# Attention rounds of a graph kernel: ten-tile stretches over three PSUM banks in place of chunks of up to four tiles

## The chip, the cores and the metric

The kernel runs on one core of one Trainium2 chip, as a single launch. The time is the device time of that launch in microseconds. Four engines take part in the stage that is changed: VectorE (DVE) does the arithmetic, GpSimd (POOL) issues the gathers, ScalarE (ACT) does the exponentials and the index arithmetic, SyncE (SP) resets signals. TensorE is idle there.

## The reference

Four graph layers follow each other over 6250 nodes of 128 features and 106250 edges (50000 drawn edges in both directions and one self loop per node): two SAGE convolutions with batch norm, a Moebius-addition scan, an equivariant convolution and a graph attention layer, with a layer norm after each. The change lies in the last one:

```python
h = (x @ W_lin).reshape(n, H, C)                    # H = 4 heads of C = 32
alpha = a_src[src2] + a_dst[dst2] + a_e
alpha = jnp.where(alpha >= 0, alpha, NEG * alpha)
m = jax.ops.segment_max(alpha, dst2, num_segments=n)
ex = jnp.exp(alpha - m[dst2])
denom = jax.ops.segment_sum(ex, dst2, num_segments=n)
w = ex / denom[dst2]
msg = h[src2] * w[:, :, None]
out = jax.ops.segment_sum(msg, dst2, num_segments=n)
```

and after it bias, residual and two layer norms.

## The kernel before

The function `gat` computes this layer in the last fifth of the launch (from about 5776 us). The nodes lie in 49 tiles of 128, one node per partition. The nodes were ordered so that those with many edges stand in the first tiles. The tiles form eight groups of 1, 4, 4, 8, 10, 9, 7 and 6 (`SIZES`), and `UPTO` holds their running sums 1, 5, 9, 17, 27, 36, 43, 49.

The work goes in turns. In one turn every node takes its next edge: POOL gathers one row of 136 floats (128 of `h`, the attention terms behind them) per node, one indirect DMA per tile, into `rows[:, r]`. There are two such buffers, r = 0 and 1, which alternate from turn to turn. As nodes run out of edges the turns get shorter: a phase p works on the first T = UPTO[p] tiles, from 49 down to 1. In the profiled execution there were twelve turns of 49 tiles, two each of 43, 36, 27, 17 and 9, four of 5 and ten of 1, which makes 882 gathers. After the phases of 49, 43, 36 and 27 tiles the group that has just ended is finished (`finish`: the self loop, division, two layer norms), on DVE and ACT.

Within a turn DVE (`turn`) first computes the scores of the gathered edges and the running maximum in small instructions (L2637 to L2649), ACT takes two exponentials into PSUM (`ex`: the factor for the old sums and the weight of the new edge), and DVE then updates `acc`, the running sum of messages. This is done in chunks of up to four tiles within a group (`CHUNKS`): 15 of them for 49 tiles. Each chunk takes three wide instructions: L2668 multiplies the old sum in `acc` by `ex[0]`; L2669 multiplies the gathered rows by `ex[1]` and writes one PSUM bank of six (`ps[:, 1 + c % 6]`); L2661 (`add_up`) adds that bank to `acc`. `add_up` of a chunk is issued one chunk later, after the two products of the next one, and waits for the signal of its own L2669.

Signals set the order. `gathered[r][g]` counts the gathers of a group, and DVE waits for all groups of the phase before a turn. `idx_ready[r]` tells POOL that ACT has the indices of the next turn in this buffer. `consumed[r][g]`, one per buffer and group, is raised by the last L2669 of a group; POOL waits for it before it gathers that group of the next turn into the same buffer (L2535 to L2539). SP clears these signals and raises each once at the start. A helper, `Chain`, raises a signal of its own after an instruction and waits for it where the next one depends on it (`do(...)` does both, `do.put` only the first).

Of the kernel before, what the change touches and what calls it, by code (L numbers as in the profile page):

```python
# [21 lines left out]
ALU = mybir.AluOpType  # L22
# [6 lines left out]
D = 128  # L29
TILES = -(-N // P)  # L30
# [33 lines left out]
NG = len(SIZES)  # L64
# [3 lines left out]
CHUNKS_TO = tuple(sum(1 for c in CHUNKS if c[0] <= g) for g in range(NG))  # L68
# [2372 lines left out]
def gat(nc, a, t, s, out):  # L2441
# [4 lines left out]
    with ExitStack() as ctx:  # L2446
# [11 lines left out]
        idx = sb("idx", [P, 2, TILES], I32)  # L2458
        MOST = max(SIZES)
        FINISH = [(g, 0, PART[g]) for g in range(NG - 1, 2, -1)] + [(0, 1, slice(0, UPTO[2]))]  # L2460
        INSIDE = NG - 4
# [28 lines left out]
        gathered = [[sem(f"gathered{r}_{g}") for g in range(NG)] for r in range(2)]  # L2490
        consumed = [[sem(f"consumed{r}_{g}") for g in range(NG)] for r in range(2)]
        scattered = sem("scattered")
# [6 lines left out]
        @block.sync  # L2499
        def _(sp):  # L2500
            for r in range(2):
                for g in range(NG):
                    sp.sem_inc(consumed[r][g], 1)
            sp.dma_start(own_row[:], t["own"].rearrange("(t p) f -> p t f", p=P)).then_inc(nodes_in, 16)
            for tile, name in ((bias, "bias"), (gain, "ln_g"), (shift, "ln_b")):
                sp.dma_start(tile[:], a["L3_gnn_" + name].partition_broadcast(P)).then_inc(w_in, 16)
            with sp.Fori(0, span_count(sp, s)) as c:
                sp.wait_ge(arrived, 3 * c + 3)
                sp.sem_inc(took, 1)
                for x in (*per_span, *consumed[0], *consumed[1]):  # L2510
                    sp.sem_clear(x)  # L2511
                for r in range(2):
                    for g in range(NG):
                        sp.sem_inc(consumed[r][g], 1)  # L2514
                sp.sem_inc(go, 1)

        @block.gpsimd
        def _(pool):
# [8 lines left out]
            with pool.Fori(0, span_count(pool, s)) as c:  # L2527
                for p, lo, hi in phases(turn_counts(pool, s)):
                    with pool.Fori(lo, hi) as b:
                        for r in range(2):  # L2530
                            pool.wait_ge(idx_ready[r], b + 1)
                            pool.sem_inc(took, 1)
                            for g in range(p + 1):
                                pool.wait_ge(consumed[r][g], b + 1)
                                pool.sem_inc(took, 1)  # L2535
                                for n in range(PART[g].start, PART[g].stop):
                                    pool.indirect_dma_start(rows[:, r, n, :], None, flat,  # L2537
                                                            bass.IndirectOffsetOnAxis(ap=idx[:, r, n:n + 1], axis=0)
                                                            ).then_inc(gathered[r][g], 16)  # L2539
# [75 lines left out]
        def _(dve):  # L2615
# [9 lines left out]

            last = [c for c, x in enumerate(CHUNKS) if c + 1 == len(CHUNKS) or CHUNKS[c + 1][0] != x[0]]

            def turn(before, p, b, r):
# [23 lines left out]
                do(dve.tensor_tensor(ex[:, 1, 0:T], ex[:, 1, 0:T], valid4, ALU.mult))  # L2652
                made = {}

                def add_up(c):
                    g, lo, hi = CHUNKS[c]
                    if c in last:
                        dve.wait_ge(consumed[r][g], b + 2)
                    else:
                        dve.wait_ge(do.sem, made[c])  # L2660
                    return dve.tensor_tensor(acc[:, lo:hi], acc[:, lo:hi],  # L2661
                                             ps[:, 1 + c % 6, 0:(hi - lo) * D].rearrange("p (u d) -> p u d", d=D), ALU.add)

                for c in range(CHUNKS_TO[p]):
                    g, lo, hi = CHUNKS[c]
                    wide = [P, hi - lo, heads, cols]
                    mine = acc[:, lo:hi].rearrange(by_head, c=cols)
                    dve.tensor_tensor(mine, mine, ex[:, 0, lo:hi].unsqueeze(3).broadcast_to(wide), ALU.mult)  # L2668
                    weighted = dve.tensor_tensor(ps[:, 1 + c % 6, 0:(hi - lo) * D].rearrange("p (u h c) -> p u h c", h=heads, c=cols),  # L2669
                                                 rows[:, r, lo:hi, 0:D].rearrange(by_head, c=cols),  # L2670
                                                 ex[:, 1, lo:hi].unsqueeze(3).broadcast_to(wide), ALU.mult)
                    if c in last:
                        weighted.then_inc(consumed[r][g], 1)
                    else:
                        do.put(weighted)
                        made[c] = do.n
                    if c == 0:
                        dve.tensor_tensor(dn, dn, ex[:, 1, 0:T], ALU.add)
                    else:
                        add_up(c - 1)  # L2680
                do(add_up(CHUNKS_TO[p] - 1))

# [157 lines left out]
```

## Time and profile before

| What | Value |
|---|---|
| Median of three runs | 7172.02 us (7158.86 to 7176.2) |
| The profiled execution | 7217.74 us, its span 7216.0 us |
| DVE busy over the span | 3417.0 us, 9467 instructions |
| POOL busy over the span | 4476.8 us, 4570 instructions |
| L2668, L2669 and L2661 | 278 instructions each |
| L2537, the gathers | 882, 851.9 us busy |

How to read it: busy time is the time in which an engine executes; time in which an instruction waits for a signal stands as idle time before it. The profile names what ended such a wait by the signal that moved last, so a signal that an earlier stage used under another name can be called by that stage's name (`mb_rows`, `eq_xrow`), and "remote" and "issue" mean that no instruction of the profile was found for it. All times within the span count from the first instruction.

### The profile page before, as it was taken

Reading aid. Unit: us, or ns where it says so; the run is one execution under the profiler, and the core shown is the slowest. Engines: PE = TensorE matmul, PEld = TensorE weight load, DVE = VectorE, ACT = ScalarE, POOL = GpSimd, SP = SyncE. Lnnn points to the kernel's source line nnn. Section 1 sums busy time; section 2 is a strip of 40 time slices with the busy share of each in tenths; the row PEclk is TensorE's granted clock in tenths of the full one; section 3 lists DMA queues with packets and bytes.
Section 4 is the critical chain, followed back from the end, with each engine's and each line's share of the span. In section 5 each row is a group of like instructions: output and inputs, shape, how many; then the busy total and the mean of one; then the engine's idle time right before and its main releaser. Section 6 shows DMA issues by size and latency. Waiting matters only on the chain. (4 is left out here: it accounts for less than half of the span.)

```text
span 7216.0 us, 54797 instructions
## 1 busy us (share of the span) xinstructions
PE 2423.7 (34%) x12640; PEld 1803.1 (25%) x12640; DVE 3417.0 (47%) x9467; ACT 1775.5 (25%) x5753; POOL 4476.8 (62%) x4570
## 2 busy tenths in 40 slices
PE   5786665465566550000000024555555300000000
PEld 4565555344444430000000012333333200000000
DVE  2333333333434363566677865555544333434466
ACT  1111111111111010222333246766666200000011
POOL 5666666566766656566665436666666577667545
PEclk7767767677778775555555557777777655555555
DMA  3333333765555523121211113333333232122111
GB/s 100 99 102 99 99 102 100 174 189 168 167 165 163 164 72 78 40 47 43 47 43 43 29 63 90 88 95 96 97 94 95 83 89 52 45 49 52 39 34 37
DMA packets 404902, 637.30 MB, mean 88 GB/s; under 512 B 148580, under 2 KB 248966, under 8 KB 404340
## 3 DMA queue, kind: packets, MB, share of 16 engines
q0 software_dynamic: 175664, 424.09, 22.4%
q1 hardware_dynamic: 139076, 115.67, 6.0%
q10 hardware_dynamic: 89856, 94.18, 4.0%
q8 instruction: 104, 1.70, 0.1%
q14 instruction: 202, 1.65, 0.1%
HBM read 529.65 MB, written 103.93 MB: 88 GB/s over the span
## 5 line engine op out<-in xcount | busy, mean ns | idle before, releaser
L1590 POOL DMA_INDIRECT mb_rows<-x_tab,mb_idx x882 | 834.4, 946 | 594.1 <-ACT mb_ps L1638 299.5
L2537 POOL DMA_INDIRECT gt_rows<-h_tab,gt_idx x882 | 851.9, 966 | 499.9 <-issue 274.0
L977 POOL DMA_INDIRECT s_rows<-y_split,srcS x824 | 857.2, 1040 | 425.9 <-issue 223.0
L2040 POOL DMA_INDIRECT eq_ring<-fx_tab,srcS x824 | 820.9, 996 | 452.8 <-issue 236.2
L555 POOL DMA_INDIRECT s_rows<-in_x,srcS x824 | 782.1, 949 | 449.6 <-issue 221.2
L2075 ACT ACTIVATE eq_ring<-eq_ring 128x64 f32<-128x64 f32 x3328 | 861.9, 336 | 459.4 <-issue 364.2
L2116 PE MATMUL eq_ps<-eq_ring,eq_onehot 128*128 128x320 f32 x1664 | 627.3, 537 | 627.1 <-issue 394.8
L2116 PEld LDWEIGHTS eq_ps<-eq_ring,eq_onehot 128*128 128x128 f32 x1664 | 381.3, 239 | 851.7 <-issue 781.8
L1700 PE MATMUL mb_ps<-ident,mb_rows 128*128 128x128 f32 x49 | 11.3, 332 | 1576.2 <-ACT mb_rows L1667 1575.3
L1055 PE MATMUL s_ps<-s_onehot,s_rows 128*128 128x128 bf16 x4992 | 444.4, 250 | 199.5 <-issue 177.6
L194 DVE TENSOR_TENSOR s_onehot<-iota,dstM 128x512 bf16<-128x512 f32 x206 | 142.4, 692 | 755.6 <-remote 389.9
L194 DVE TENSOR_TENSOR s_onehot<-s_ps,dstM 128x512 f32<-128x512 f32 x206 | 141.9, 689 | 716.9 <-PE s_ps L630 431.1
L1055 PEld LDWEIGHTS s_ps<-s_onehot,s_rows 128*128 128x128 bf16 x4992 | 380.2, 114 | 286.0 <-issue 247.6
L629 PE MATMUL s_ps<-s_onehot,s_rows 128*128 128x128 f32 x1664 | 424.5, 390 | 1.6 <-DVE s_onehot L194 1.6
L1638 ACT ACTIVATE mb_ps<-mb_rows,mb_gm 128x128 f32<-128x128 f32 x882 | 260.9, 351 | 601.0 <-DVE mb_gm L1789 524.5
L1700 PEld LDWEIGHTS mb_ps<-ident,mb_rows 128*128 128x128 f32 x49 | 6.8, 154 | 1580.8 <-issue 1573.6
L629 PEld LDWEIGHTS s_ps<-s_onehot,s_rows 128*128 128x128 f32 x1664 | 365.8, 260 | 61.8 <-issue 22.4
L2661 DVE TENSOR_TENSOR gt_acc<-gt_acc,gt_ps 128x128 f32<-128x128 f32 (+3 forms) x278 | 158.6, 574 | 400.3 <-remote 171.4
L1749 DVE TENSOR_TENSOR mb_prod<-mb_ps,mb_xf 128x256 f32<-128x256 f32 (+3 forms) x278 | 276.1, 1000 | 127.0 <-issue 36.3
L1741 DVE TENSOR_REDUCE mb_both<-mb_prod 128x2 f32<-128x256 f32 (+3 forms) x278 | 275.4, 994 | 61.2 <-DVE mb_prod L1749 29.6
L1804 DVE SCALAR_TENSOR_TENSOR mb_xf<-mb_xf,mb_v,mb_ps 128x128 f32<-128x128 f32 x882 | 247.8, 343 | 101.5 <-issue 51.7
L194 DVE TENSOR_TENSOR eq_onehot<-eq_ps,dstM 128x512 f32<-128x512 f32 x206 | 141.6, 687 | 317.9 <-remote 228.9
(505 smaller groups left out, 5484.1 us busy)
## 6 DMA issues: line engine op xcount, KB each, us to landing
w_tab<-s_wrow ACTq DMA_DIRECT2D x208, 264.0 KB
eq_ring<-w_tab SPq DMA_DIRECT2D x208, 264.0 KB
s_es<-in_side ACTq DMA_DIRECT2D x208, 136.0 KB
mb_rows<-x_tab,mb_idx POOLq DMA_INDIRECT x882
gt_rows<-h_tab,gt_idx POOLq DMA_INDIRECT x882
s_rows<-in_x,srcS POOLq DMA_INDIRECT x824
s_rows<-y_split,srcS POOLq DMA_INDIRECT x824
eq_ring<-fx_tab,srcS POOLq DMA_INDIRECT x824
```

Of the source, the lines that this page charges most:

```text
L194: return dve.tensor_tensor(onehot[:, 4 * half:4 * half + 4], broadcast(numbers, four, 1), broadcast(columns, four, 2), ALU.is_equal)
L555: pool.indirect_dma_start(rows[:, n % SLOTS, :], None, a["x"], bass.IndirectOffsetOnAxis(ap=s["srcS"][:, n:n + 1], axis=0)).then_inc(gathe ...
L629: pe.matmul(ps[:, bank, 0:P], rows[:, slot], onehot[:, u], start=(u == 0), stop=(u == U - 1))
L977: pool.indirect_dma_start(rows[:, n % SLOTS, :], None, t["ys"], bass.IndirectOffsetOnAxis(ap=s["srcS"][:, n:n + 1], axis=0)).then_inc(gath ...
L1055: last = pe.matmul(ps[:, 2 * bank + f, 0:P], rows[:, slot, at:at + P], onehot[:, u], start=(u == 0 and part == 0), stop=(u == U - 1 and pa ...
L1590: pool.indirect_dma_start(rows[:, r, n, :], None, t["x1"], bass.IndirectOffsetOnAxis(ap=idx[:, r, n:n + 1], axis=0)).then_inc(gathered[r][ ...
L1741: do.put(dve.tensor_reduce(both[:, :, lo:hi], prod[:, c % 3, :, 0:hi - lo], AX_X, ALU.add))
L1749: dve.tensor_tensor(prod[:, c % 3, :, 0:hi - lo], copied(c).unsqueeze(1).broadcast_to(wide), xf[:, :, lo:hi, 0:D], ALU.mult).then_inc(mult ...
L2040: pool.indirect_dma_start(frow[:, n % SLOTS, :], None, features, bass.IndirectOffsetOnAxis(ap=s["srcS"][:, n:n + 1], axis=0)).then_inc(gat ...
L2075: last = act.activation(pb[:, r % 2, u, f].rearrange("p c w -> p (c w)"), wrow[:, r, u, lo:lo + 64], ACT.Copy, scale=wrow[:, r, u, D + f:D ...
L2116: last = pe.matmul(ps[:, bank, 0:MC], onehot[:, 4 * h + u], msg[:, h, u], start=(h == 0 and u == 0), stop=(h == 1 and u == 3))
L2537: pool.indirect_dma_start(rows[:, r, n, :], None, flat, bass.IndirectOffsetOnAxis(ap=idx[:, r, n:n + 1], axis=0)).then_inc(gathered[r][g], 16)
```

## The change

It concerns `turn` and the signals it shares with POOL and SP. In place of the 15 chunks a turn has stretches of ten tiles (`RUN`), regardless of the groups: five for 49 tiles, the last of nine. A stretch takes three PSUM banks, 1 to 3 or 4 to 6 in turn. The order of the three wide instructions stays as it was; in each the operand in PSUM now stands first. `consumed` is kept per stretch, not per group, and every L2669 raises it; POOL waits for it before the first tile of each stretch. From the third stretch on, the product into PSUM waits until the addition of the stretch before last, which read the same banks, is done.

```diff
+        RUN = 10
+        RUNS = -(-TILES // RUN)
...
-        consumed = [[sem(f"consumed{r}_{g}") for g in range(NG)] for r in range(2)]
+        consumed = [[sem(f"consumed{r}_{c}") for c in range(RUNS)] for r in range(2)]
...
                             for g in range(p + 1):
-                                pool.wait_ge(consumed[r][g], b + 1)
-                                pool.sem_inc(took, 1)
                                 for n in range(PART[g].start, PART[g].stop):
+                                    if n % RUN == 0:
+                                        pool.wait_ge(consumed[r][n // RUN], b + 1)
+                                        pool.sem_inc(took, 1)
...
-                made = {}
-
-                def add_up(c):
-                    g, lo, hi = CHUNKS[c]
-                    if c in last:
-                        dve.wait_ge(consumed[r][g], b + 2)
-                    else:
-                        dve.wait_ge(do.sem, made[c])
-                    return dve.tensor_tensor(acc[:, lo:hi], acc[:, lo:hi],
-                                             ps[:, 1 + c % 6, 0:(hi - lo) * D].rearrange("p (u d) -> p u d", d=D), ALU.add)
-
-                for c in range(CHUNKS_TO[p]):
-                    g, lo, hi = CHUNKS[c]
+                runs = [(c, c * RUN, min(c * RUN + RUN, T)) for c in range(-(-T // RUN))]
+                weights = lambda c, many: ps[:, 1 + 3 * (c % 2):4 + 3 * (c % 2), :].rearrange("p b n -> p (b n)")[:, 0:many * D]
+
+                def add_up(c, lo, hi):
+                    dve.wait_ge(consumed[r][c], b + 2)
+                    do.put(dve.tensor_tensor(acc[:, lo:hi], weights(c, hi - lo).rearrange("p (u d) -> p u d", d=D),
+                                             acc[:, lo:hi], ALU.add))
+                    added[c] = do.n
+
+                added = {}
+                for c, lo, hi in runs:
                     wide = [P, hi - lo, heads, cols]
                     mine = acc[:, lo:hi].rearrange(by_head, c=cols)
-                    dve.tensor_tensor(mine, mine, ex[:, 0, lo:hi].unsqueeze(3).broadcast_to(wide), ALU.mult)
-                    weighted = dve.tensor_tensor(ps[:, 1 + c % 6, 0:(hi - lo) * D].rearrange("p (u h c) -> p u h c", h=heads, c=cols),
-                                                 rows[:, r, lo:hi, 0:D].rearrange(by_head, c=cols),
-                                                 ex[:, 1, lo:hi].unsqueeze(3).broadcast_to(wide), ALU.mult)
-                    if c in last:
-                        weighted.then_inc(consumed[r][g], 1)
-                    else:
-                        do.put(weighted)
-                        made[c] = do.n
+                    dve.tensor_tensor(mine, ex[:, 0, lo:hi].unsqueeze(3).broadcast_to(wide), mine, ALU.mult)
+                    if c >= 2:
+                        dve.wait_ge(do.sem, added[c - 2])
+                    dve.tensor_tensor(weights(c, hi - lo).rearrange("p (u h c) -> p u h c", h=heads, c=cols),
+                                      ex[:, 1, lo:hi].unsqueeze(3).broadcast_to(wide),
+                                      rows[:, r, lo:hi, 0:D].rearrange(by_head, c=cols), ALU.mult).then_inc(consumed[r][c], 1)
                     if c == 0:
                         dve.tensor_tensor(dn, dn, ex[:, 1, 0:T], ALU.add)
                     else:
-                        add_up(c - 1)
-                do(add_up(CHUNKS_TO[p] - 1))
+                        add_up(*runs[c - 1])
+                add_up(*runs[-1])
+                do.sync()
```

SP clears and raises the new list of signals in the same two places as the old one.

## Rows read from the trace of the kernel before

**Rows 1.** The page's engine shares: busy us, share of the span, instructions.

```profile
PE 2423.7 (34%) x12640; PEld 1803.1 (25%) x12640; DVE 3417.0 (47%) x9467; ACT 1775.5 (25%) x5753; POOL 4476.8 (62%) x4570
```

**Rows 2.** Waits of POOL, 5776 to 7216: us in total, times, longest.

```profile
POOL gt_rows L2537 <- issue: 274.0, 851, 8.9
POOL gt_rows L2537 <- DVE gt_ps L2669: 158.9, 13, 36.2
POOL gt_rows L2537 <- DMA mb_rows<-x_tab,mb_idx: 59.3, 15, 14.1
```

**Rows 3.** Stretches, one per turn or finish: limits, length, busy us (instructions), clock, DMA.

```profile
6159.90:6242.00 82.10, 0.00 (x0) 0.00 (x0) 28.36 (x59) 0.70 (x2) 47.95 (x50) 0.50 0.19 42
6522.30:6562.40 40.10, 0.00 (x0) 0.00 (x0) 26.85 (x59) 2.07 (x3) 22.46 (x24) 0.50 0.18 41
6627.00:6710.30 83.30, 0.00 (x0) 0.00 (x0) 28.25 (x59) 0.50 (x1) 62.33 (x66) 0.50 0.24 55
6710.30:6740.30 30.00, 0.00 (x0) 0.00 (x0) 13.34 (x49) 4.47 (x11) 0.00 (x0) 0.50 0.01 2
6740.30:6765.40 25.10, 0.00 (x0) 0.00 (x0) 23.75 (x53) 4.09 (x10) 14.18 (x15) 0.50 0.17 39
6765.40:6817.80 52.40, 0.00 (x0) 0.00 (x0) 24.71 (x53) 0.46 (x1) 39.75 (x42) 0.50 0.24 56
6817.80:6857.00 39.20, 0.00 (x0) 0.00 (x0) 14.91 (x53) 4.84 (x12) 14.18 (x15) 0.50 0.12 29
6857.00:6878.70 21.70, 0.00 (x0) 0.00 (x0) 20.20 (x47) 4.29 (x11) 11.88 (x13) 0.50 0.16 38
6919.40:6954.60 35.20, 0.00 (x0) 0.00 (x0) 18.01 (x61) 5.58 (x14) 8.52 (x9) 0.50 0.08 20
6954.60:6972.60 18.00, 0.00 (x0) 0.00 (x0) 15.56 (x38) 4.83 (x13) 8.61 (x10) 0.50 0.14 31
6972.60:6994.40 21.80, 0.00 (x0) 0.00 (x0) 15.82 (x38) 0.35 (x1) 16.62 (x18) 0.50 0.25 58
6994.40:7029.10 34.70, 0.00 (x0) 0.00 (x0) 19.54 (x65) 5.91 (x15) 6.95 (x8) 0.50 0.07 16
```

**Rows 4.** The same view, two stretches of POOL's gathers.

```profile
5811.97:6027.20 215.23, 0.00 (x0) 0.00 (x0) 67.59 (x145) 4.92 (x8) 162.97 (x172) 0.50 0.24 56
6027.30:6089.90 62.60, 0.00 (x0) 0.00 (x0) 20.49 (x43) 0.28 (x1) 49.10 (x45) 0.50 0.21 50
```

**Rows 5.** DVE in order of time, a slow turn: start, us, instruction, idle before.

```profile
6085.72 0.36 DVE L2645 TENSOR_TENSOR span_src<-span_src,gt_limit 128x196 f32<-128x196 f32 x1 [2.85 <-remote]
6087.12 0.36 DVE L2646 TENSOR_TENSOR span_src<-span_src 128x196 f32<-128x196 f32 x1 [1.04 <-issue]
...
6106.73 0.69 DVE L2661 TENSOR_TENSOR gt_acc<-gt_acc,gt_ps 128x512 f32<-128x512 f32 x1 [2.31 <-DMA mb_rows<-x_tab,mb_idx]
6107.33 0.68 DVE L2668 TENSOR_TENSOR gt_acc<-gt_acc,gt_ps 128x512 f32<-128x512 f32 x1
6107.93 0.69 DVE L2669 TENSOR_TENSOR gt_ps<-gt_rows,gt_ps 128x512 f32<-128x512 f32 x1
6110.23 0.69 DVE L2661 TENSOR_TENSOR gt_acc<-gt_acc,gt_ps 128x512 f32<-128x512 f32 x1 [1.60 <-issue]
```

**Rows 6.** The same view, in a finish: three instructions of 1280 elements.

```profile
7008.23 1.50 DVE L2723 TENSOR_TENSOR gt_ps<-gt_acc,gt_ps 128x1280 f32<-128x1280 f32 x1 [0.40 <-DVE gt_ps L2722]
7009.64 1.48 DVE L2725 TENSOR_TENSOR gt_rows<-gt_own_row,gt_ps 128x1280 f32<-128x1280 f32 x1
7011.15 1.50 DVE L2727 TENSOR_TENSOR gt_ps<-gt_ps,gt_rows 128x1280 f32<-128x1280 f32 x1
```

**Rows 7.** The first gathers, and DVE's first instruction on gathered rows.

```profile
5780.74 0.99 POOL L2537 DMA_INDIRECT gt_rows<-h_tab,gt_idx  x1 [8.89 <-issue]
...
5800.83 7.09 POOL L2537 DMA_INDIRECT gt_rows<-h_tab,gt_idx  x1 [0.30 <-issue]
...
5849.74 0.36 DVE L2640 TENSOR_TENSOR span_src<-gt_rows,edges_in 128x196 f32<-128x196 f32 x1 [30.89 <-DMA gt_rows<-h_tab,gt_idx]
```

More of the change, by code:

```diff
@@ L2501, in _ @@
             for r in range(2):
-                for g in range(NG):
-                    sp.sem_inc(consumed[r][g], 1)
+                for c in range(RUNS):
+                    sp.sem_inc(consumed[r][c], 1)
             sp.dma_start(own_row[:], t["own"].rearrange("(t p) f -> p t f", p=P)).then_inc(nodes_in, 16)
@@ L2512, in _ @@
                 for r in range(2):
-                    for g in range(NG):
-                        sp.sem_inc(consumed[r][g], 1)
+                    for k in range(RUNS):
+                        sp.sem_inc(consumed[r][k], 1)
                 sp.sem_inc(go, 1)
@@ L2624, in _ @@
             by_head = "p u (h c) -> p u h c"
-            last = [c for c, x in enumerate(CHUNKS) if c + 1 == len(CHUNKS) or CHUNKS[c + 1][0] != x[0]]
             def turn(before, p, b, r):
```

## The prediction

> **What bounds the kernel now.** I read the engine shares first. Over the whole span DVE is busy 47% and POOL 62% [rows 1], which says nothing of the last stage, where alone the change lies. So next come the waits of POOL inside that stage (5776 to 7216 us). Its 882 gathers wait 274.0 us for "issue", which is the fixed 0.3 us between two gathers. The other two rows are the ones to see: 158.9 us for L2669 and 59.3 us under the name of a transfer of an earlier stage [rows 2]. By the code a gather waits only for `idx_ready` and `consumed`, so most of these 218 us is POOL waiting for DVE to release row buffers.
>
> Third comes the table of stretches, one per turn [rows 3]. A turn of 49 tiles is 59 DVE instructions with 27 to 28 us of busy time. It took 82.1 us at 6160, as in seven of the twelve such turns to within 2 us, and 40.1 us in the one at 6522. The same work, twice the time: DVE is not busy, it is held. POOL needs 49 gathers of 1.2513 us (215.23 us for 172, [rows 4]), 61.3 us a turn. So the slow turns are set by DVE, the fast ones would be set by POOL.
>
> Fourth, DVE's own sequence shows where it is held: always at an instruction that waits for one of DVE's own signals [rows 5]. The addition at 6106.73 runs 0.60 us and the next two follow at 0.60 us each. Then the addition at 6110.23 starts after 1.60 us idle, though the product it waits for had ended long before. The spacing tells the price: 3.50 us for three instructions of 0.69 us there, 1.40 us for one instruction of 0.36 us at L2645. Over the slow turn it is 82.1/59 = 1.39 us per instruction, at 6627 83.3/59 = 1.41 us. So in this state the signals come back at a rate of one instruction per 1.4 us, whatever its length. Three instructions of 1280 elements follow each other 1.41 and 1.51 us apart with no idle time before them [rows 6]: an instruction that lasts 1.4 us pays nothing extra.
>
> **The change part by part.** *Fewer, wider instructions.* A turn of 49 tiles has 15 chunks, each with three wide instructions, 45 in all. Now it has five stretches (ten, ten, ten, ten, nine tiles), 15 instructions; the 14 others stay. 29 instructions at 1.40 us are 40.6 us in the held state. Not held, the 30 that go save only their fixed part: 512 elements are 0.60 us apart [rows 5], 1280 elements 1.41 us [rows 6], so 0.81 us for 768 elements, and 0.60 - 512 x 0.81/768 = 0.06 us is fixed; 30 x 0.06 = 1.8 us off 40.1 us. Either way the turn takes about 40 us, under POOL's 61.3 us.
>
> *What is late next.* POOL. Its first gather starts at 5780.74, one early gather takes 7.09 us, 6.1 us more than the others, and DVE starts its turn some 2.8 us after the start of the last gather (the 49th starts at 5780.74 + 48 x 1.2513 + 6.1 = 5846.9, L2640 at 5849.74) [rows 7]. Twelve turns of 49 are 588 gathers; without waiting for DVE the last starts at 5780.74 + 587 x 1.2513 + 6.1 = 6521.4 and the twelfth turn can start at 6524 instead of 6627: 103 us.
>
> *From there on* I follow both engines [rows 3]. The twelfth turn takes 40.6 us instead of 83.3 us and ends at 6565; the finish of the first group (30.0 us, not touched) ends at 6595. Two turns of 43 tiles: the first (25.1 us, less 24 x 0.06) ends at 6619, but the gathers of the second end only at 6521.4 + 86 x 1.2513 + 2.8 = 6632. It takes 29 x 1.40 = 40.6 us (52.4 us before), its finish 39.2 us: 6712. Two turns of 36 (14 + 12 instructions): POOL is ready at 6722, the first ends at 6712 + 20.4 = 6732, the second at 6769, its finish (35.2 us) at 6804. Two turns of 27: 17.1 and 20.9 us, finish 34.7 us: 6877, where it was 7029.1. That is 152 us. The turns of 17 to 5 tiles lose 42 instructions in all, 2.5 us, which I leave out against the releases below; those of one tile keep theirs.
>
> *POOL's own slow stretch.* From 6027 to 6090 45 gathers took 62.6 us, 1.39 us each [rows 4], after 215 us without a pause. Nothing in the rows tells why. POOL will now run for 740 us without a pause, so I charge one such stretch per 278 us, 2.7 x 45 x 0.14 = 17 us. At both ends: none, and all gathers (rival one).
>
> *Coarser releases.* `consumed` is now signalled per ten tiles, the first after two instructions of 1280 elements (2.8 us) instead of two of 128 (0.5 us or less). In turns of 49 POOL is a whole buffer behind these signals, 61.3 us against 40.6 us, so this is hidden; if that cover is gone it costs 2.3 us at each of the 28 waits of [rows 2]. In the eight turns of 17 to 5 tiles, where POOL and DVE alternate, it costs 0 to 2 us each; I take nothing, set against the 2.5 us.
>
> *Operand order, three banks.* The PSUM operand goes from second to first. L2723 and L2725 have it second, L2727 has it first: 1.50, 1.48 and 1.50 us for 1280 elements over three banks [rows 6]. Nothing, within 0.02 us x 15 a turn either way. The new wait for the bank of the stretch before last has a 1.4 us product issued in front of it and only the product behind it; held, it is one of the 29 instructions already counted. Six signals fewer to clear and set on SP: outside the turns, nothing.
>
> Sum: 152 - 17 = 135 us off the profiled execution's 7217.7 us (span 7216.0 us): 7083 us. The median of the runs, 7172.0 us, lies 45.7 us under it; with that difference kept it is 7037 us, and I say 7040 us. If the 45.7 us are delays that the timed runs never had, the gain is smaller by up to as much, 7083 us.
>
> One rule speaks against this. The row shows a wait for the own signal costing 1.0 to 2.3 us idle [rows 5]. The Trainium skill (VectorE: DVE Perf Modes, The DRAIN you can't avoid) says that a semaphore after each instruction costs nothing beyond the drain and that only the count of instructions matters, by their fixed part. By that the sum would be rival two's; the rows of this stage disagree.
>
> **The rivals.** *One: POOL falls to 1.39 us for good.* For: it did so in one long unpaused stretch [rows 4]. Against: it came back without a pause. The last gather of 49 tiles then starts at 5780.74 + 587 x 1.39 + 6.1 = 6602.8, the second turn of 43 at 6725, and by the same steps the finish after the turns of 27 ends near 6969: 60 us off, 7112 us.
>
> *Two: the hold does not go with the number of instructions* but with POOL's gathers beside it, so slow turns stay near 80 us. For: the turn at 6522 began after POOL had paused. Against: short and long instructions pay the same 1.4 us. Then only the fixed part goes, 1.8 us in seven slow turns of 49 and 10 us in the later ones (162 instructions): 7149 us.
>
> *Three: the hold belongs to the recording.* Starts after waits lie 0.70 us or a multiple apart (1.40 and 3.50 us, [rows 5]), as if timed by a clock outside the kernel. Then the timed runs are set by POOL already, and the change gains 10 us in the late turns: 7162 us. Against: without the hold the profiled execution would be well over 100 us shorter, yet it is only 45.7 us above the runs. The Trainium skill (NOTIFIC — the notification-queue block, 7.1) says that the block which writes trace records holds its producers back rather than lose a record; no run here shows whether it does.
>
> *Four, slower: the releases decide.* If slow turns stay as in rival two and POOL's restarts lie on the path, each of the 28 waits lengthens by 2.3 us, 64 us, less the 23 us of rival two: 7213 us. It decides from the point where a turn of DVE takes longer than POOL's 61.3 us. Against: 29 instructions would each have to cost over 2.1 us.
>
> **How the numbers follow.** Forecast 0.60 (7005 to 7085), rival one 0.20, two 0.08, three 0.06, four 0.06. The range 7005 to 7125 holds the first two, 0.80. About 0.3%, 21.5 us, can be told from no change. Faster: the first two and most of two, 0.86. Same: three and the rest of two, 0.08. Slower: four, 0.06.
>
> **What would show it.** Right: turns of 49 tiles 61 to 62 us apart, 29 DVE instructions in each, no idle time of POOL for L2669's successor before the last gather of 49 tiles, and the first finish starting near 6565 us. Wide instructions 1.4 us apart, without idle time before the additions. Rival one shows in a mean gather spacing near 1.39 us; two in turns still near 80 us with idle time before the five additions; three in a profile much faster than before and a median that has hardly moved; four in pauses of POOL at every first tile of a turn. The prediction is wrong if DVE turns of 49 tiles still take longer than 61 us.

## The result and the profile after

Over seven runs each the kernel after takes 7121.57 us (7111.88 to 7139.59), the kernel before 7161.19 us (7146.09 to 7176.2): ratio 0.9946, interval 0.9932 to 0.996, a gain of 39.6 us. I had forecast 7040 us (7005 to 7085), 132 us below 7172. The direction was right, the size three times too large.

The two profiles, 7216.0 and 7117.8 us long, are 98.2 us apart, more than the runs. The gathers show why. These are the first gathers of the last stage, first in the profile of after, then in a later profile of the same kernel (start, us, instruction, idle before):

```profile
5725.62 0.99 POOL L2540 DMA_INDIRECT gt_rows<-h_tab,gt_idx  x1 [8.91 <-issue]
```

```profile
5774.69 0.99 POOL L2540 DMA_INDIRECT gt_rows<-h_tab,gt_idx  x1 [8.93 <-issue]
```

Before starts there at 5780.74 [rows 7]. So 55.1 of the 98.2 us lie ahead of the changed code and are the chip's, as the second row shows: on that chip before takes 7212 us, on the first 7161 us. From the first gather to the end before takes 7216.0 - 5780.7 = 1435.3 us, after 7117.8 - 5725.6 = 1392.2 us: 43.1 us less, which agrees with the runs. From here on times count from the first gather.

The page's shares, to be read against [rows 1]: 522 DVE instructions fewer, 50 us less DVE work, and POOL 59 us busier with the same 4570 instructions.

```profile
PE 2464.8 (35%) x12640; PEld 1819.3 (26%) x12640; DVE 3367.3 (47%) x8945; ACT 1782.4 (25%) x5753; POOL 4535.9 (64%) x4570
```

The waits of the stage (total us, times, longest), against [rows 2]:

```profile
DVE span_src L2641 <- DMA gt_rows<-h_tab,gt_idx: 484.0, 16, 43.6
POOL gt_rows L2540 <- issue: 284.0, 868, 8.9
POOL gt_rows L2540 <- DVE gt_ps L2670: 103.4, 11, 32.9
```

The roles have changed: DVE now waits 484.0 us for gathers, and POOL's waits for DVE (158.9 us and 59.3 us before) are 103.4 us and all lie behind the turns of 49 tiles. Stretches of after, to be read with [rows 3, 4] (limits, length, then PE, PEld, DVE, ACT, POOL busy with instructions, clock, DMA): the second, fourth, fifth and sixth batch of 49 gathers, then the first finish, two turns of 43, the second finish, two turns of 36, the third finish.

```profile
5793.26:5854.59 61.33, 0.00 (x0) 0.00 (x0) 25.10 (x29) 2.07 (x3) 46.39 (x50) 0.50 0.25 56
5916.05:5977.43 61.38, 0.00 (x0) 0.00 (x0) 25.09 (x29) 2.07 (x3) 46.44 (x49) 0.50 0.25 56
5977.43:6045.34 67.91, 0.00 (x0) 0.00 (x0) 25.03 (x29) 0.79 (x2) 52.12 (x49) 0.50 0.22 50
6045.34:6114.48 69.14, 0.00 (x0) 0.00 (x0) 24.96 (x29) 2.07 (x3) 53.09 (x49) 0.50 0.22 49
...
6553.00:6616.10 63.10, 0.00 (x0) 0.00 (x0) 13.45 (x49) 4.52 (x11) 48.29 (x46) 0.50 0.23 50
6616.10:6655.80 39.70, 0.00 (x0) 0.00 (x0) 22.32 (x29) 4.15 (x10) 31.16 (x29) 0.50 0.22 49
6655.80:6696.30 40.50, 0.00 (x0) 0.00 (x0) 22.40 (x29) 0.46 (x1) 30.96 (x30) 0.50 0.23 50
6696.30:6770.80 74.50, 0.00 (x0) 0.00 (x0) 14.91 (x53) 4.87 (x12) 40.14 (x37) 0.50 0.16 35
6770.80:6792.90 22.10, 0.00 (x0) 0.00 (x0) 18.88 (x27) 4.43 (x11) 9.31 (x10) 0.50 0.13 29
6792.90:6812.50 19.60, 0.00 (x0) 0.00 (x0) 18.81 (x26) 0.42 (x1) 14.72 (x17) 0.50 0.23 53
6812.50:6858.30 45.80, 0.00 (x0) 0.00 (x0) 18.24 (x61) 5.61 (x15) 27.23 (x29) 0.50 0.20 46
```

Two things stand out. The first four batches take 61 us (the first 68, with a long gather as in [rows 7]); from the fifth on every batch takes 67.9 to 69.2 us in the turns of 49, a mean of 1.40 us per gather. And the first finish, 49 instructions with 13.4 us of work, takes 63.1 us where it took 30.0 us. In the row of before POOL has 0.00 us beside it; here it has 46 gathers. DVE inside the second finish, in order of time (start, us, idle before):

```profile
6719.29 1.49 DVE L2699 BATCH_NORM_STATS2 gt_stats<-gt_ps 128x6 f32<-128x128 f32 x7 [0.30 <-DVE gt_ps L2725]
6728.39 0.58 DVE L2702 BATCH_NORM_AGGREGATE gt_mv<-gt_stats 128x2 f32<-128x6 f32 x7 [7.62 <-issue]
6738.19 0.17 DVE L2704 TENSOR_SCALAR gt_var<-gt_mv 128x7 f32<-128x7 f32 x1 [9.22 <-issue]
```

Seven short statistics (1.49 us together) are followed 9.10 us after their start, seven aggregations (0.58 us) 9.80 us after theirs: 1.3 and 1.4 us for each instruction. POOL, late in the turns of 49:

```profile
6353.88 0.94 POOL L2540 DMA_INDIRECT gt_rows<-h_tab,gt_idx  x1 [0.30 <-issue]
6355.13 0.95 POOL L2540 DMA_INDIRECT gt_rows<-h_tab,gt_idx  x1 [0.30 <-issue]
6356.38 0.99 POOL L2540 DMA_INDIRECT gt_rows<-h_tab,gt_idx  x1 [0.30 <-issue]
6357.68 1.10 POOL L2540 DMA_INDIRECT gt_rows<-h_tab,gt_idx  x1 [0.30 <-issue]
6359.08 1.09 POOL L2540 DMA_INDIRECT gt_rows<-h_tab,gt_idx  x1 [0.30 <-issue]
6360.48 1.80 POOL L2540 DMA_INDIRECT gt_rows<-h_tab,gt_idx  x1 [0.30 <-issue]
6362.58 1.10 POOL L2540 DMA_INDIRECT gt_rows<-h_tab,gt_idx  x1 [0.30 <-issue]
```

The gathers start 1.25 us apart, then 1.40, once 2.10 us. The last row is tile 30, the only one ahead of which the program lets POOL wait for `consumed`; without that wait the same tile is just as late (e4_one_wait, below).

### The profile page after: what moved, and what is told of

It is laid out like the page before. It is cut to its first block and busy times, and to the rows that moved or that the text cites. A ratio compares the mean times of both kernels' runs of the same rounds, so it can differ in the third digit from the quotient of the medians.

```text
span 7117.8 us, 54197 instructions
## 1 busy us (share of the span) xinstructions
PE 2464.8 (35%) x12640; PEld 1819.3 (26%) x12640; DVE 3367.3 (47%) x8945; ACT 1782.4 (25%) x5753; POOL 4535.9 (64%) x4570
## 5 line engine op out<-in xcount | busy, mean ns | idle before, releaser
L2540 POOL DMA_INDIRECT gt_rows<-h_tab,gt_idx x882 | 913.3, 1035 | 395.6 <-issue 284.0
L2116 PEld LDWEIGHTS eq_ps<-eq_ring,eq_onehot 128*128 128x128 f32 x1664 | 382.1, 239 | 826.9 <-issue 758.1
L1055 PE MATMUL s_ps<-s_onehot,s_rows 128*128 128x128 bf16 x4992 | 471.3, 255 | 243.1 <-issue 226.6
L2233 DVE TENSOR_TENSOR eq_ring<-eq_ring 128x512 f32<-128x512 f32 x208 | 143.4, 689 | 281.6 <-DMA fx_tab<-mb_rows,perm 180.1
```

Source lines behind the costliest of these rows:

```text
L1055: last = pe.matmul(ps[:, 2 * bank + f, 0:P], rows[:, slot, at:at + P], onehot[:, u], start=(u == 0 and part == 0), stop=(u == U - 1 and pa ...
L2116: last = pe.matmul(ps[:, bank, 0:MC], onehot[:, 4 * h + u], msg[:, h, u], start=(h == 0 and u == 0), stop=(h == 1 and u == 3))
L2540: pool.indirect_dma_start(rows[:, r, n, :], None, flat, bass.IndirectOffsetOnAxis(ap=idx[:, r, n:n + 1], axis=0)).then_inc(gathered[r][g], 16)
```

## The experiments

My theory after the comparison: beside POOL's gathers DVE gets through one instruction per 1.40 us, and POOL itself, after a first reserve of gathers at its own 1.25 us, one gather per 1.40 us; each counts instructions, not work, signals or bytes. An engine that does not get its next instruction through although its data are there I call held. The rivals: the limit goes with signals, with waits, with one rate that both engines share, or with the transfers.

**Operand order alone (e1_before_psum_first).**

```
-  acc[:, lo:hi], acc[:, lo:hi], ps[...], ALU.add
+  acc[:, lo:hi], ps[...], acc[:, lo:hi], ALU.add      (and so in the two products)
```

> The kernel before with one part of the change alone: the three wide VectorE instructions have their PSUM operand first; the 15 chunks, banks and signals stay as they were. If operand order costs nothing, as the prediction took it, the time is that of the kernel before, 7161 us within 0.3%, and the 512-element instructions stay 0.60 us apart where nothing holds them. If the order carried part of the measured gain, it is between 7121 and 7150 us. Its profile also tells whether the profiled execution of before (7217.7 us) was typical: if it was, turns of 49 tiles again take 82 us in seven of twelve; if not, fewer are held.

Measured 7212.89 us against 7213.78 us, ratio 0.9999 (0.9989 to 1.0008): operand order is worth nothing. Its first gather starts at 5779.7 us and a held turn takes 82.1 us, as in the profile of before. So that profile was typical of this chip; the expected 7161 us were another chip's.

**Fewer signals (e2_last_signal).**

```
-  for u in range(many): do.put(dve.bn_stats(...))
-  do.sync()
+  for u in range(many): one = dve.bn_stats(...)
+  do(one)                                             (bn_aggr likewise)
```

> The kernel after, with a semaphore signal only on the last bn_stats and the last bn_aggr of each group of the finishes (the first finish issues 50 instructions on DVE as before, 24 of them lose their signal). Theory signals: DVE is held 1.4 us for every signal it sends while POOL gathers beside it; then the first finish falls from 62.7 us to about 40 us and the second from 74.0 to about 45 us, and the time to about 7070 us. Theory count: what is limited is the number of instructions (POOL's and DVE's together), signal or not; then the first finish stays at 60 to 65 us and the time at 7121 us within 0.3%.

The first finish of this kernel, as a stretch:

```profile
6611.39:6674.39 63.00, 0.00 (x0) 0.00 (x0) 13.39 (x49) 4.45 (x11) 48.17 (x46) 0.50 0.21 50
```

63.00 us with 20 signals fewer (24 is the count of the second finish, which takes 74.5 us as in after): the hold counts instructions, not signals. The time, 7171.66 us, ratio 0.9931 (0.9914 to 0.9948), is that of after on this chip (0.9938, below).

**Shorter stretches (e3_run5).** `RUN = 10` becomes `RUN = 5`.

> The kernel after with stretches of five tiles: 30 wide instructions in a turn of 49 tiles instead of 15, 44 DVE instructions in all instead of 29. Theory shared budget: late in the stage gathers and DVE instructions draw on one rate, and from the held turns (49 gathers with 29 instructions in 68.6 us, 49 with 59 in 80.2 us) a DVE instruction costs 0.39 us although POOL is the later engine; then held turns take 74.4 us and the time is about 7121 + 8 x 5.8 + some 5 in the later turns = 7172 us. Theory two rates: POOL falls to 1.39 us a gather for its own reasons and DVE, at 44 x 1.40 = 61.6 us, stays under it; then held turns stay at 68 to 69 us and the time at 7121 us, or 10 us more for the fixed parts in the late turns.

A late batch of 49 gathers, and the first finish:

```profile
6020.74:6088.66 67.92, 0.00 (x0) 0.00 (x0) 26.57 (x44) 0.79 (x2) 51.87 (x50) 0.50 0.22 50
...
6611.03:6679.93 68.90, 0.00 (x0) 0.00 (x0) 13.38 (x50) 4.56 (x12) 52.85 (x50) 0.50 0.21 49
```

POOL's batch takes 67.92 us with 44 DVE instructions beside it, as with 29: DVE's instructions do not slow POOL, and my fit of 0.39 us per DVE instruction falls. The ratio, 0.9962 (0.9948 to 0.9976), lies a little above that of after, with intervals that overlap; in the profiles the first finish ends 20 us later, as told below, and the stage is 16 us longer (1410.1 us against 1393.8).

**One wait a turn (e4_one_wait).** POOL waits for `consumed` once, ahead of a turn's first gather, instead of per ten tiles.

> The kernel after, with POOL waiting once a turn for the last stretch released (one wait and one count of it instead of five of each). In the held turns the gather at such a wait comes 2 to 3 us after the one before instead of 1.25 to 1.40. If the waits cost POOL that, the 8 held turns of 49 tiles lose 4 waits of about 1.2 us each and the turns of 43 some more: about 7080 us. If the rate is set elsewhere and the waits only show where it is felt, held turns stay at 68 to 69 us and the time at 7121 us; the coarser release can add up to 2 us in each of the eight turns of 17 to 5 tiles.

7179.92 us, ratio 0.995 (0.9934 to 0.9967); a late batch takes 67.9 us again, and tile 30 starts 2.10 us after tile 29 without its wait too. In the turns of 49 the waits cost nothing. The stage is 7 us longer than in after (1400.7 us), all of it behind those turns.

**After, on the same chip (e5_after_again).**

> The kernel after, unchanged, on the chip of the other experiments, so that profiles of one chip are compared. Two profiles of the kernel before and four others start their first gather of the last stage at 5769 to 5784 us, the profile of after at 5725.6 us: the difference of 45 to 58 us arises ahead of the code that was changed. If that is the chip's, this run starts it near 5776 us too, and its profile ends near 7172 us; from the first gather on it takes 1392 us as in the first profile of after (1435 us before), and the ratio is 0.994 to 0.996. If the early stages were faster by the change itself, the first gather starts near 5726 us here too, and the ratio stands at 0.987 or below.

First gather at 5774.69 us, 7165.79 us, ratio 0.9938 (0.9917 to 0.9958). The 55 us belong to the chip.

**POOL stopped during the first finish (e6_pause).**

```
+  if (p, r, n) == (NG - 2, 0, 20):
+      pool.wait_ge(normed[0], 2)
```

> The kernel after, where POOL waits ahead of its 21st gather for the first turn of 43 tiles until the first finish has ended: POOL stands still while DVE does that finish. Theory beside: DVE's 1.4 us per instruction holds only while POOL gathers beside it, late in its unbroken run; then the first finish takes 30 us again instead of 62.8, and a pause also gives POOL its 1.25 us a gather back, so that the second finish, beside a fresh POOL, is nearer 39 us than 74 and the time falls by 20 to 45 us below that of after. Theory finish itself: something in the changed kernel makes the finishes longer whatever POOL does; then the first finish stays at 60 us or more and the time grows by up to 30 us through the pause.

The first finish, two batches of gathers behind the pause, and the second finish:

```profile
6670.48:6731.84 61.36, 0.00 (x0) 0.00 (x0) 29.67 (x36) 0.73 (x2) 46.43 (x49) 0.50 0.24 56
6731.84:6793.02 61.18, 0.00 (x0) 0.00 (x0) 22.58 (x52) 4.29 (x10) 46.25 (x49) 0.50 0.24 56
6595.50:6631.40 35.90, 0.00 (x0) 0.00 (x0) 13.34 (x49) 4.49 (x11) 0.41 (x1) 0.50 0.01 2
6740.90:6812.20 71.30, 0.00 (x0) 0.00 (x0) 14.90 (x54) 4.89 (x13) 49.70 (x53) 0.50 0.23 53
```

With POOL still the same finish takes 35.90 us instead of 63.1: the hold of DVE goes away without gathers, but not at once. POOL's last gather starts at 6594.81 us of the span. Two stretches of the finish behind it:

```profile
6597.50:6622.50 25.00, 0.00 (x0) 0.00 (x0) 6.50 (x21) 1.53 (x2) 0.00 (x0) 0.50 0.00 0
6622.50:6631.40 8.90, 0.00 (x0) 0.00 (x0) 5.74 (x21) 2.96 (x9) 0.00 (x0) 0.50 0.00 0
```

21 instructions take 25.0 us although POOL stands still and no transfer runs; the next 21 take 8.9 us. So neither gathers in the making nor their transfers can be what holds DVE there; when the hold ends is worked out at the end of this section. POOL's pace comes back for 98 gathers. But the second finish takes 71.30 us beside a POOL at 1.25 us a gather, so DVE's hold does not need POOL to be slow; that part of my expectation was wrong. The time, 7173.91 us (0.9951, 0.9933 to 0.9969), did not fall: the gathers that the pause put off came later.

**DVE's work taken out (e7_product_only).**

> The kernel after without the scaling of the sums and without the additions in the turns: of the 15 wide instructions of a turn of 49 tiles only the five products stay, 19 DVE instructions instead of 29 (its sums are not built). Theory own pace: POOL's fall from 61.4 to 68 to 69 us for 49 gathers, after 196 gathers without a pause, does not hang on DVE; then the fifth and later batches of 49 gathers again take 67.9 and 69.1 us by turns. Theory shared: DVE's instructions and POOL's gathers draw on one rate; then with ten instructions fewer a turn the fall comes later than after 196 gathers or the batches take 65 us or less.

The fourth to sixth batch of 49 gathers:

```profile
5969.16:6030.90 61.74, 0.00 (x0) 0.00 (x0) 11.34 (x19) 2.07 (x3) 46.80 (x49) 0.50 0.24 55
6030.90:6098.67 67.77, 0.00 (x0) 0.00 (x0) 11.42 (x19) 0.79 (x2) 52.27 (x50) 0.50 0.22 50
6098.67:6167.98 69.31, 0.00 (x0) 0.00 (x0) 11.35 (x19) 2.07 (x3) 52.91 (x49) 0.50 0.21 49
```

With less than half of DVE's work POOL falls at the same gather to the same pace. It is POOL's own. The single run took 7146.82 us.

**Fewer instructions in the finishes (e8_few_in_finish).**

```
-  per tile: bn_stats, bn_aggr
+  tensor_reduce(sums); tensor_copy; tensor_tensor(square); tensor_reduce(square); four small ones
```

> The kernel after, where the finishes take mean and variance by eight wide instructions for all tiles (two sums, a copy, a square, four small ones) instead of one bn_stats and one bn_aggr per tile: the first four finishes issue 40 DVE instructions each instead of 50, 54, 62 and 66, of about the same busy time. Theory count: late in the stage a finish costs 1.25 to 1.4 us per instruction whatever it does; then the first falls from 62.8 to about 50 us and the second from 74.2 to about 54 us, and the time by 20 to 35 us below that of after. Theory work: the finishes are longer because each instruction runs slower beside the gathers, in proportion to its work; then both stay within 4 us of 62.8 and 74.2 us, and the time with them.

First finish, second finish, two turns of 36:

```profile
6598.23:6647.53 49.30, 0.00 (x0) 0.00 (x0) 18.04 (x39) 4.50 (x11) 36.84 (x36) 0.50 0.21 50
6728.53:6783.44 54.91, 0.00 (x0) 0.00 (x0) 20.48 (x40) 4.94 (x13) 42.33 (x40) 0.50 0.21 50
6783.44:6819.53 36.09, 0.00 (x0) 0.00 (x0) 18.95 (x26) 4.34 (x11) 18.39 (x18) 0.50 0.14 33
6819.53:6855.93 36.40, 0.00 (x0) 0.00 (x0) 18.91 (x26) 0.41 (x1) 25.90 (x29) 0.50 0.23 52
```

49.3 and 54.9 us, as the count says, though their work grew from 13.4 to 18.0 us and from 14.9 to 20.5. Yet the time did not move: 7166.84 us, 0.994 (0.9919 to 0.9961). The two turns of 36 tiles behind them now run beside 47 gathers instead of 27 and take 36.1 and 36.4 us instead of 22.1 and 19.6. They give back nearly all of the 33 us. Into the first of them POOL stands still for 32.87 us in after, here for 12.26 us.

**Two pauses in the turns of 49 (e9_pauses).** Ahead of the fifth and ninth turn:

```
+  pool.wait_ge(consumed[1][0], at + 1)                (at = 2, 4)
```

> The kernel after, where POOL stops twice in the twelve turns of 49 tiles: ahead of the fifth and of the ninth it waits until DVE has released the first stretch of the turn before, about 10 us after the last gather of that turn started, so about 9 us without a gather each time. Theory unbroken run: POOL falls from 1.25 to 1.39 us a gather after some 250 us without a pause and a pause gives 1.25 back (after the one of the first finish 98 gathers took 61.4 and 61.2 us per 49); then all twelve batches of 49 take 61 to 62 us except for the pauses, the first finish starts at about 827 - 8 x 7.2 + 2 x 9 = 787 us after the first gather, and the time is some 40 us below that of after, ratio about 0.988. Theory too short: pauses of 9 us give nothing back; then batches of 68 to 69 us follow them and the time is 18 us above that of after.

Four batches of 49 gathers, the first with the pause in it:

```profile
5912.69:5983.83 71.14, 0.00 (x0) 0.00 (x0) 32.85 (x45) 2.86 (x5) 46.37 (x49) 0.50 0.21 49
5983.83:6045.11 61.28, 0.00 (x0) 0.00 (x0) 17.15 (x14) 0.00 (x0) 46.34 (x49) 0.50 0.24 55
6045.11:6110.82 65.71, 0.00 (x0) 0.00 (x0) 25.11 (x29) 2.07 (x3) 48.91 (x49) 0.50 0.23 52
6110.82:6178.88 68.06, 0.00 (x0) 0.00 (x0) 24.97 (x29) 0.78 (x2) 52.27 (x50) 0.50 0.22 50
```

Together 266.2 us; without the pause the same four batches take 61.4 + 67.9 + 69.1 + 68.1 = 266.5 us. A pause gives back its own length and no more. So both theories failed: the first finish starts at 826.4 us, neither earlier nor later than in after (827.4). Ratio 0.9948 (0.9932 to 0.9965), on a chip where before takes 7162.64 us.

**Stretches of 25 tiles (e10_run25).** `RUN = 25`, one buffer of seven banks, the addition ahead of the next product.

> The kernel after with stretches of 25 tiles over seven banks in one buffer: 6 wide instructions in turns of 49 and 43 tiles instead of 15, 20 DVE instructions instead of 29, and two waits of POOL a turn instead of five. POOL sets the turns of 49 tiles at 67.9 and 69.1 us, so nothing is gained there. In the turns of 43 tiles, which run held between the finishes, nine instructions fewer are worth up to 10 us each by the count; the last experiment's gain in the finishes was taken back by the turns behind them, so by theory given back the time stays within 8 us of that of after, ratio 0.993 to 0.995; by theory count alone it falls by 20 us, ratio 0.991.

The first finish, unchanged in itself:

```profile
6565.86:6616.66 50.80, 0.00 (x0) 0.00 (x0) 13.35 (x49) 4.51 (x12) 38.73 (x37) 0.50 0.22 51
```

It is 12.3 us shorter because the turn ahead of it has nine instructions fewer. Ratio 0.9937 (0.9921 to 0.9954): in part given back, as in the experiment on the finishes: the first finish ends 13.7 us earlier than in after, the stage 7.8 us (1386.0 against 1393.8 us).

**Short pauses (e11_short_pauses).** At the same places POOL waits for its own last gathers only.

> The kernel after, where POOL stops at the same two places only until its own last gathers have landed, some 2.8 us after the last one started: about 1.5 to 2 us without a gather each time. If a pause this short gives POOL its 1.25 us back, the first finish starts near 827 - 8 x 7.2 + 2 x 2 = 774 us after the first gather and the ratio is near 0.986. If a pause must be longer, as it must if some backlog of hundreds of gathers has to drain, batches stay at 68 to 69 us, the first finish starts at 827 to 832 us and the time is that of after, ratio 0.993 to 0.995.

First finish at 826.9 us, ratio 0.9946 (0.993 to 0.9963): no gain from a pause of 2 us either.

**All three together (e12_combined).**

> The kernel after with three changes together: the two pauses ahead of the fifth and ninth turn (here about 13 us, since the first stretch has 25 tiles), stretches of 25 tiles, and finishes with eight wide instructions for mean and variance. If the pauses give POOL's pace back and the fewer instructions shorten the finishes (62.8 to 49, 74.2 to 54 us) without all being taken back, the first finish starts near 795 us after the first gather and the ratio is 0.984 to 0.989, the fastest of all; if the pauses give nothing, it is 0.994 to 0.998.

The first finish:

```profile
6556.57:6593.37 36.80, 0.00 (x0) 0.00 (x0) 18.39 (x40) 4.54 (x12) 27.23 (x27) 0.50 0.22 50
```

7108.66 us against 7162.64 us, ratio 0.9923 (0.9907 to 0.994), the lowest of all (its interval overlaps those of after), though not by the pauses: the first finish starts at 826.2 us again. It ends at 863.0 us instead of 890.7 by having 19 instructions fewer in its turn and itself, and 17 us of that last to the end of the stage (1376.7 us against 1393.8, one profile each).

**What POOL's limit counts (e13_half_row, e14_half_rows).** `rows[:, r, n, HW // 2:HW]`, and `rows[0:64, r, n, :]` with `idx[0:64, ...]`, as the gather's target.

> The kernel after, where each gather brings half of the row's bytes (272 instead of 544 for each of 128 rows; the other half of the buffer is zeroed once ahead of the stage, some 10 to 20 us, and its sums are not those of the graph). If POOL's limit counts instructions or rows, the first four batches of 49 gathers take 61 to 62 us and the fifth and later ones again 67.9 and 69.1 us. If it counts bytes, or if the transfers set it, the later batches stay near 61 us and the first finish starts near 790 us after the first gather instead of 827.

> The kernel after, where each gather brings 64 rows instead of 128 (same bytes per row; the other half of the buffer is zeroed once ahead of the stage; its sums are not those of the graph). A gather alone may then be shorter than 1.25 us. If the limit counts instructions, batches of 49 settle at 49 x 1.40 = 68.6 us all the same, once what POOL has in hand is used up, and a shorter gather only uses it up earlier. If it counts rows, it lies at 0.70 us a gather and POOL never meets it: turns of 49 tiles take the gather's own pace or DVE's 29 x 1.40 = 40.6 us, and the first finish starts 200 to 330 us earlier than in after.

Half of each row: a late batch. Then half of the rows: the third to fifth batch.

```profile
5995.64:6063.71 68.07, 0.00 (x0) 0.00 (x0) 24.95 (x29) 0.79 (x2) 51.70 (x50) 0.50 0.15 25
```

```profile
5863.02:5922.17 59.15, 0.00 (x0) 0.00 (x0) 24.99 (x29) 0.79 (x2) 44.22 (x49) 0.50 0.16 29
5922.17:5991.28 69.11, 0.00 (x0) 0.00 (x0) 24.89 (x29) 2.07 (x3) 51.69 (x50) 0.50 0.13 25
5991.28:6059.19 67.91, 0.00 (x0) 0.00 (x0) 24.95 (x29) 0.79 (x2) 51.73 (x50) 0.50 0.13 25
```

Half the bytes (25 instead of 50 GB/s, last column) or half the rows leave 68 to 69 us. With half the rows a gather alone is shorter, 59.15/49 = 1.207 us, and the fall comes one batch earlier, after 147 gathers instead of 196. That is what a reserve of instructions does: 196 x (1 - 1.2513/1.40) = 20.8 and 147 x (1 - 1.207/1.40) = 20.3 gathers ahead of one per 1.40 us. The limit counts gathers, not rows or bytes. In both kernels the first finish starts at 829 us (827.4 in after); each ran once, 7137.85 and 7136.33 us beside 7147.15 us for before.

DVE's side comes out of the same runs. Instructions in the twelfth turn and the first finish, and when the finish starts and ends, in us from the first gather:

```
kernel                   turn + finish   starts   ends
after (e5)                  29 + 49       827.6   890.7
e8_few_in_finish            29 + 39       827.4   876.7
e10_run25                   20 + 49       826.2   877.0
e7_product_only             19 + 49       814.1   876.7
e12_combined                20 + 39       826.2   863.0
e3_run5                     44 + 49       841.9   910.8
```

In all six DVE has the gathers for that turn at 801 to 802 us. From 59 to 93 instructions the end moves by 47.8 us, 1.41 us for each, whichever they are; 78 x 1.40 - (890.7 - 802) = 20 us, some 15 instructions, are DVE's reserve. (The first finish has 49 instructions, 39 in e8_few_in_finish, one fewer than my expectations say.)

The traces also tell when DVE's hold ends. Let POOL's lead be the number of gathers that it is ahead of one per 1.40 us: each gather adds one, every 1.40 us takes one off, never below none. In the late turns of 49 of after it stays at 20 to 21. When POOL stops, it takes lead x 1.40 us to run off. Six stops of POOL, in us from the start of the span (an estimate, worked out from the starts of all gathers):

```
kernel, finish     last gather   lead   lead run off   DVE's last held start
before, first          6709.3    15.1         6730.5                  6726.2
before, second         6835.5     8.5         6847.3                  6847.7
e6_pause, first        6594.8    21.7         6625.1                  6622.5
after, second          6746.2    21.6         6776.4                  6773.9
after, third           6847.3     6.5         6856.4                  6856.2
after, fourth          6908.5     4.5         6914.8                  6914.6
```

The last held start is the last one after an idle time of 0.9 us or more that neither ACT nor a gather explains. It lies between 4.3 us ahead of the moment when the lead has run off and 0.4 us behind it. So DVE is held as long as POOL's lead lasts, not only while POOL gathers. It fits that the two turns of 36 ran free in after, where POOL had stood still for 32.87 us, and not in e8_few_in_finish after 12.26 us. This was read from the traces afterwards; no run varied the lead alone.

## Why the prediction was wrong

My sum was -135 us in the stage, measured are -43.1 us. Step by step, in us (the 17 us charged for slow stretches are in the first row; the last finish makes up the rest):

```
                                           forecast   measured   miss
first finish starts                          -128      -102.1     +26
four finishes (139.1 before, 219.2 after)       0       +80.1     +80
turns of 43, 36 and 27 (179.5 to 154.4)        -7       -25.1     -18
turns of 17 and fewer                           0        +4.6      +5
```

*Turns of 49 tiles: right.* 29 instructions, 25 us of work, DVE waits for the gathers, POOL sets the pace; 61.3 us a turn is right for four turns.

*"POOL's own slow stretch ... I charge one such stretch per 278 us, 17 us": the first step that failed.* I took the 45 slow gathers of [rows 4] for an episode. They were the normal state after the reserve is used up. Then a gather costs 1.40 us, and before left that state only because DVE made POOL wait. The 588th gather started at 799.2 us where the forecast had 587 x 1.2513 + 6.1 = 741 us: 59 us instead of 17. The last turn of 49 gave 15 us back, since DVE, idle before it, needed 25 us and not 40.6. Rival one had this mechanism, and with 7112 us is the nearest number; it got 0.20 because POOL "came back without a pause". But the waits of [rows 2] were pauses. That its number is so near is partly luck: by its steps the first finish would start at 865 us, 38 us too late, and it too left the finishes at their old length, 80 us too short.

*"The finish of the first group (30.0 us, not touched)", and 39.2, 35.2 and 34.7 us likewise: the second and larger.* I applied 1.40 us per instruction to the turns alone. The finishes have 49, 53, 61 and 65 instructions; the first two now cost 63.1 and 74.5 us. The row that told it was in my hands: 30.0 us with POOL at 0.00 (x0) [rows 3]. Even there DVE was held until 6726.2 us of the span, while POOL's lead ran off. An untouched part keeps its duration only with its neighbours. That, too, is why fewer instructions in the finishes alone won nearly nothing: while POOL's lead lasts, DVE, its reserve spent, gets 1.40 us per instruction wherever it stands, and what one part saves the next one pays.

*The reading of the hold.* "The signals come back at a rate" was wrong in its first word: without 20 to 24 signals nothing changes. The Trainium skill (VectorE: DVE Perf Modes, The DRAIN you can't avoid), which I had set aside on this, says that a semaphore costs nothing extra; that agrees with the 63.00 us. The three instructions of [rows 6], from which I took it that one of 1.4 us pays nothing extra, start at 7008.2 us of the span, where POOL's lead has just run off (by the same working, at 7008.7): they showed little of the held state. That turns of 43 came out as counted (29 instructions in 39.7 us, 15 of them wide) was partly luck. Rival two, which tied the hold to the gathers beside it, had half of the truth; its price, turns that stay near 80 us, was wrong.

*The 45.7 us* between the profile of before and the median were the chip's. Keeping the difference was right. My remark that the gain might shrink by it falls, and so does rival three's forecast, timed runs that hardly move; whether the recording is what holds the engines is another question, below. Operand order costs nothing, as forecast (e1_before_psum_first); of the coarser releases and the banks no cost shows, but no run took them singly; rival four did not appear.

What holds both engines to 1.40 us is not settled. The Trainium skill (NOTIFIC — the notification-queue block, 7.1) tells of a block whose internal pipeline holds its producers back rather than lose a trace record inside it. One instruction per fixed time, whatever it does, and a lead that has to run off would fit, but that is not shown: no run here was without records. Gathers and transfers in flight are ruled out for DVE by the 25.0 us beside a POOL that stands still, DVE's work for POOL by e7_product_only.

## What to carry to other kernels

Where an engine runs at a steady spacing that its instructions' length doesn't explain, count instructions over a long stretch, on each engine, and test whether any stretch of the trace ever beats that rate for longer than a reserve; a fast beginning is no proof of the pace. Before taking an untouched part at its old duration, look at what ran beside it in the row, and ask whether the change puts something else there. A saving that only moves where two engines meet is largely paid back behind it; only fewer instructions in all, on the engine that is held, lasted here, 17 us of 28 in the best version. And where an engine stands still, look how long its neighbour stays slow behind it: that tells a store that runs off from a clash of the two.

## What the runs showed of the hardware that I had not expected

- POOL sustains one gather per 1.40 us (67.9 and 69.1 us for 49, by turns) with a reserve of some 20; bytes, rows, waits and DVE's work change nothing in that, and pauses of 2 to 9 us return only themselves.
- DVE sustains one instruction per 1.40 us beside gathers, with a reserve of some 15. The hold outlasts POOL's last gather until POOL's lead has run off: 25.0 us for 21 instructions with POOL standing still, then 8.9 us for 21 (e6_pause).
- Two chips differ by some 45 us in the stages ahead of the change (first gather at 5723 to 5743 us and at 5768 to 5784 us), with the same durations in this stage: profiles of two chips are to be compared from the start of the changed stage on.
